# Attention passes of one width, ordered high before low, with two transposes of the second head moved between

## The chip, the cores and the metric

The kernel runs on one core of a Trainium2 chip. The metric is the device time of one execution in microseconds (us); lower is better. TensorE (PE) does matmuls and transposes, VectorE (DVE), ScalarE (ACT) and GpSimd (POOL) the elementwise work; SyncE (SP) issues most transfers.

## The reference

Eight sequences of 512 tokens by 256 channels go through a selective state-space layer (stage A of the kernel), then through attention whose value and output projections are sums over experts chosen by a gate (stage B), then through a feed-forward part and norms (stage C). The change is in stage B, which computes this, in float32:

```python
# x: (b, s, 256); 16 heads, 64 values a head, 8 experts of which 2 are kept
q = _rope(einsum('bsd,hdp->bhsp', x, Wq)); k = _rope(einsum('bsd,hdp->bhsp', x, Wk))
gv = _gate(x, Wsel_v)
v = einsum('bsd,bhse,hedp->bhsp', x, gv, Wv)
att = softmax(einsum('bhsp,bhtp->bhst', q, k) / sqrt(P), axis=-1)
o = einsum('bhst,bhtp->bhsp', att, v)
go = _gate(x, Wsel_o)
return einsum('bhsp,bhse,hepd->bsd', o, go, Wo)
```

## The kernel before

Every engine has its own program, written out by hand; semaphores tie them together, and each engine works strictly in the order of its own program. Stage B (`stage_b`, from line 875) runs 8 pairs of heads by 8 sequences, 64 batches. `turns` loops over them; `it` is the batch's number, `j` the pair and `b` the sequence. The last sequence of a pair also prepares the next pair's weights, and the first one comes right after them.

To keep float32 precision with a faster matmul type, each operand is split into a high part (rounded) and a low part (what rounding left). A product is three matmuls: high by high, high by low and low by high (`product`, L1156 to L1158). ScalarE makes the high parts and VectorE or GpSimd the low ones, always after the high one.

One batch, in TensorE's order (`batch`, L1255): the values of both heads' experts (`values`) mixed with the scores (`scores`); the transposes of head 0's exponentiated scores, four groups of four 128x128 transposes (`turn_probabilities`, L1200, groups n = 0 to 3, one PSUM bank each); head 0's attention (`attend`, L1210); head 1's transposes, n = 4 to 7, in the same four banks; the transposes of the output gates (`turn_gates`); head 1's attention; eight gate matmuls (`spread_gates`, L1233) with the next batch's raw query and key projection between them (`project_raw`); and 48 matmuls of output projection (`project`). The first gate matmul waits for the gates' low part (`low_gates`, L1462). The output projection waits for the low part of the first gated output, which GpSimd makes (`low_outputs`, L1060).

Attention of a head is four key chunks c, each with a high and a low pass over 512 queries. `vv` holds a head's values per chunk: 64 columns of high parts, then 64 of low parts. The high pass (L1219) has all 128 columns as weights and streams the high part of the probabilities, so its bank holds high by high on partitions 0 to 63 and low by high on 64 to 127. The low pass (L1221, for the last chunk L1218 and ahead of the high pass) has the 64 high columns and streams the low part. `attend` waits once per chunk, for the chunk's low part. Then ScalarE moves one half of the bank beside the other (`move_part`, L1342, into `aside`), and VectorE adds them (`add_parts`, L1469, into `oT`). Only then do the outputs of both heads get their gates (`gate_outputs`, L1478), go to ScalarE for the high part (L1353) and to GpSimd for the low part.

The order around this on the other engines: ScalarE does the high copies of head 0 (`high_probabilities`, L1331, n = 0 to 3), the next batch's input (`high_x`), head 1's values (`high_values`, L1325), `move_part` of head 0, then the high copies of head 1 (n = 4 to 7), the gates' high part (L1335) and `move_part` of head 1. VectorE does the gated values, the low parts of head 0 (`low_probabilities`, L1454), the output gates, `add_parts` of head 0, the low parts of head 1, `low_gates`, `add_parts` of head 1 and the gated outputs. A copy of head 1 into the ring of four chunks waits for the pass that read the old chunk (`pv_psum`).

Of the kernel before, what the change touches and what calls it, by code (L numbers as in the profile page):

```python
# [15 lines left out]
F32, F32R = mybir.dt.float32, mybir.dt.float32r  # L16
ALU = mybir.AluOpType
ACT = mybir.ActivationFunctionType
AX = mybir.AxisListType

P = 128
NB, S, D = 8, 512, 256
TT = S // P
# [6 lines left out]
H, E, HP, F = 16, 8, 64, 1024  # L30
# [844 lines left out]
def stage_b(nc, d, const, acc):  # L875
# [6 lines left out]
    with ExitStack() as ctx:  # L882
        def sb(name, shape, dtype=F32):
            return ctx.enter_context(nc.sbuf_tensor(name, shape, dtype))
# [7 lines left out]
        ps = ctx.enter_context(nc.psum_tensor("ps_b", [P, 8, S], F32))  # L892
# [23 lines left out]
        qk_full = sb("qk_full", [P, 2, S])  # L916
# [1 line left out]
        vg = sb("vg", [P, TT, E, HP])  # L918

        v4 = qk_full[:, :, :].rearrange("p a s -> p (a s)").rearrange("p (t e n) -> p t e n", t=TT, e=E // 2)  # L920
        oT, aside = sb("oT", [P, S]), sb("aside", [P, S])
        v2 = sb("v2", [P, TT, E // 4, HP])
        v = sb("v", [P, 2, TT, HP])
        vv = sb("vv", [P, 2, TT, 2 * HP], F32R)
        negmax = sb("negmax", [P, TT, 2])
        total = sb("total", [P, 2, TT])
        share = sb("share", [P, 2, TT])
# [3 lines left out]
        RING = 4  # L931
        probT = parts("probT", [P, RING, S])
# [5 lines left out]
        consts_loaded, consts_done, zero_done = sem("consts_b_loaded"), sem("consts_b_done"), sem("zero_done")  # L938
# [6 lines left out]
        v_psum, vg_done, vsum_done = sem("v_psum"), sem("vg_done"), sem("vsum_done")  # L945
        v_high, v_low = sem("v_high"), sem("v_low")
# [66 lines left out]
        def turns(eng, start, batch, pair_start=None):  # L1013

            def pair(j, more):
                if pair_start:
                    pair_start(j)
                with eng.Fori(0, NB - 1) as b:
                    batch(j * NB + b, j, b, True, False)
                batch(j * NB + (NB - 1), j, NB - 1, False, more)  # L1020

            start()
            with eng.Fori(0, PAIRS - 1) as j:
                pair(j, True)
            pair(PAIRS - 1, False)

        @block.gpsimd
        def _(pool):
            def low_x(it):
                pool.wait_ge(xT_high, it + 1)  # L1030
                pool.tensor_tensor(xT[1][:, :, :], xT_in[:, :, :], xT[0][:, :, :].bitcast(F32), ALU.subtract).then_inc(xT_low, 1)
# [20 lines left out]

            def low_values(it, h):
                pool.wait_ge(v_high, it * 2 + h + 1)
                pool.tensor_tensor(vv[:, h, :, HP:2 * HP], v[:, h, :, :], vv[:, h, :, 0:HP].bitcast(F32), ALU.subtract).then_inc(v_low, 1)

            def low_outputs(it, e):

# [85 lines left out]
                    rank_four(it + 1, ahead)  # L1144

            pool.memset(out_gate[:, :, :], 0.0).then_inc(zero_done, 1)
            low_x(0)

            pool.dma_start(acc[:, :, :, :], d["xT"].rearrange("b p k s -> p b k s")).then_inc(acc_loaded, 16)
# [3 lines left out]
        def _(pe):  # L1153
# [39 lines left out]
            def turn_probabilities(it, n):  # L1193
                h, c = divmod(n, TT)
                if n in (0, 3):
                    pe.wait_ge(exp_done, it * 2 * TT + (7 if n == 0 else 8))
                elif n >= 4:
                    pe.wait_ge(pT_low, it * N + n - 3)
                for t in range(TT):
                    mm = pe.transpose(ps[:, c, t * P:(t + 1) * P], prob[h][:, t, c * P:(c + 1) * P], ident[:, :])  # L1200
                mm.then_inc(pT_psum, 1)
# [5 lines left out]
                    mm = pe.transpose(ps[:, GT_BANK, t * P:(t + 1) * P], out_gate[:, t, :], ident[:, :])  # L1207
                mm.then_inc(gT_psum, 1)

            def attend(it, h, c):  # L1210

                if c == 0:
                    pe.wait_ge(v_low, it * 2 + h + 1)
                n = h * TT + c
                pe.wait_ge(pT_low, it * N + n + 1)
                bank, last = ATTEND_BANK[h], c == TT - 1
                if last:
                    pe.matmul(ps[0:HP, bank, :], vv[:, h, c, 0:HP], probT[1][:, n % RING, :], start=False, stop=False)  # L1218
                mm = pe.matmul(ps[:, bank, :], vv[:, h, c, :], probT[0][:, n % RING, :], start=(c == 0), stop=last)  # L1219
                if not last:  # L1220
                    mm = pe.matmul(ps[0:HP, bank, :], vv[:, h, c, 0:HP], probT[1][:, n % RING, :], start=False, stop=False)  # L1221
                mm.then_inc(pv_psum, 1)

            def spread_gates(it, p):

# [29 lines left out]
            def batch(it, j, b, more, more_pairs):  # L1255
                pe.wait_ge(w_low["wv"], j * 2 + 2)
                values(it, 0, 0)
                values(it, 0, 1)
                scores(it, 0)
                scores(it, 1)  # L1260
                values(it, 0, 2)
                values(it, 0, 3)
                values(it, 1, 0)
                scores(it, 2)
                scores(it, 3)
                values(it, 1, 1)
                values(it, 1, 2)
                values(it, 1, 3)
                for n in range(TT):
                    turn_probabilities(it, n)  # L1270
                for c in range(TT):
                    attend(it, 0, c)
                for n in range(TT, N):
                    turn_probabilities(it, n)
                turn_gates(it)
                for c in range(TT):
                    attend(it, 1, c)
                spread_gates(it, 0)
                spread_gates(it, 1)
                if more or more_pairs:  # L1280
                    if more_pairs:
                        pe.wait_ge(w_low["wqk"], j + 2)
                    project_raw(it + 1, 0)
                spread_gates(it, 2)
                if more or more_pairs:
                    project_raw(it + 1, 1)
                spread_gates(it, 3)
                for n in range(N):
                    project(it, j, n)

            pe.wait_ge(consts_done, 1)
            turns(pe, start, batch)

        @block.scalar
        def _(act):
# [26 lines left out]

            def high_values(it, h):
                act.wait_ge(vsum_done, CREDIT + it * VSUM + h * 6 + 6)
                act.activation(vv[:, h, :, 0:HP], v[:, h, :, :], ACT.Copy).then_inc(v_high, 1)  # L1325

            def high_probabilities(it, n):
                act.wait_ge(pT_psum, it * N + n + 1)
# [8 lines left out]
            def move_part(it, h):  # L1337

                act.wait_ge(pv_psum, it * N + h * TT + TT)
                act.wait_ge(oT_done, it * 2 + h)  # L1340
                here, other = slice(h * HP, (h + 1) * HP), slice((1 - h) * HP, (2 - h) * HP)
                act.activation(aside[here, :], ps[other, ATTEND_BANK[h], :], ACT.Copy).then_inc(part_moved, 1)  # L1342

# [59 lines left out]
        def _(dve):  # L1403
# [12 lines left out]
            def rotate(it):  # L1416

                dve.wait_ge(vsum_done, CREDIT + it * VSUM)
                dve.wait_ge(rot_done, it * 3 + 3)
                dve.tensor_tensor(qk_full[:, :, :], rot[:, 0:2, :], rot[:, 2:4, :], ALU.add).then_inc(qk_done, 1)  # L1420

# [134 lines left out]

            dve.wait_ge(tables_loaded, 32)
            dve.wait_ge(consts_done, 1)
            dve.wait_ge(zero_done, 1)
            turns(dve, start, batch)  # L1560


# [397 lines left out]
```

## Time and profile before

| what | value |
|---|---|
| median of 3 runs (lowest, highest) | 4069.31 us (4068.82, 4069.96) |
| the profiled execution's own time | 4069.74 us |
| its span, first to last instruction | 4067.9 us |
| TensorE busy, mean granted clock | 3706.3 us (91%), 0.972 |
| VectorE busy | 3307.9 us (81%) |
| GpSimd busy | 2717.1 us (67%) |
| ScalarE busy | 1962.4 us (48%) |

How to read it: busy time is the time in which an engine has an instruction in work. Matmuls overlap (a 512-column matmul is recorded as 0.39 us but the next one starts 0.23 later), so starts tell more than durations. A timeline row gives the start in us from the beginning, the duration (of a run of equal instructions, from the first start to the last end), the engine (PEld is TensorE's weight load), the line, the operation, output<-inputs, shapes and the count; in brackets the idle time before it and what ended it.

### The profile page before, as it was taken

The page shows a single profiled execution, that of the slowest core. Times are in us where ns is not written, and L with a number is a line of the kernel's source. Part 1 is how long each engine was busy: PE and PEld are TensorE (multiplying, and loading weights), DVE is VectorE, ACT ScalarE, POOL GpSimd, SP SyncE. Part 2 cuts the span into 40 slices and gives each one's busy share as a digit, 9 for nine tenths or more (in the row PEclk, how much of TensorE's full clock was granted, in tenths as well). Part 3 has the DMA queues.
Part 4 walks back from the last instruction along what each step waited for, and adds up shares of the span by engine and source line. Part 5 has one row for each costly group of instructions (what it writes and reads, how often), then busy time and mean ns, then how long its engine had stood idle before and what let it go on. Part 6 is the DMA issues. An engine that isn't in the chain of part 4 may idle for free. (4 is left out here: it accounts for less than half of the span.)

```text
span 4067.9 us, 55014 instructions
## 1 busy us (share of the span) xinstructions
PE 3706.3 (91%) x16000; PEld 2539.0 (62%) x16000; DVE 3307.9 (81%) x3879; ACT 1962.4 (48%) x3646; POOL 2717.1 (67%) x2844
## 2 busy tenths in 40 slices
PE   6888988888649999999999999999999999999786
PEld 2344434443337777777777777777777777777675
DVE  5999999999928787878787878778788778787698
ACT  4645664566324444454445454545454445444443
POOL 3767776777636677667667667667667667766354
PEclk9999999999969999999999999999999999999898
DMA  2101110111030001001001001001000000000111
GB/s 75 52 37 37 63 68 37 37 62 63 21 134 16 10 16 39 15 15 39 13 18 37 12 10 44 15 10 44 10 15 17 37 10 21 11 15 10 33 41 36
DMA packets 53667, 131.92 MB, mean 32 GB/s; under 512 B 4223, under 2 KB 33791, under 8 KB 47073
## 3 DMA queue, kind: packets, MB, share of 16 engines
q1 hardware_dynamic: 52560, 127.02, 8.7%
q0 software_dynamic: 1040, 4.19, 0.3%
q8 instruction: 20, 0.33, 0.0%
q14 instruction: 47, 0.38, 0.0%
HBM read 114.16 MB, written 17.04 MB: 32 GB/s over the span
## 5 line engine op out<-in xcount | busy, mean ns | idle before, releaser
L371 POOL TENSOR_TENSOR state<-state,c_rows 128x1024 f32<-128x1024 f32 x256 | 604.1, 2363 | 266.8 <-DVE state L790 265.5
L1320 ACT ACTIVATE prob<-ps_b,negmax 128x512 f32<-128x512 f32 x512 | 345.8, 686 | 653.1 <-DVE negmax L1439 653.1
L790 DVE TENSOR_TENSOR_SCAN state<-dA,ps_a 128x1024 f32<-128x1024 f32 x256 | 584.6, 2284 | 29.9 <-PE ps_a L503 7.9
L503 PE MATMUL ps_a<-state,ident 128*128 128x512 f32 x1024 | 504.7, 617 | 70.9 <-DVE yz L802 70.5
L666 ACT ACTIVATE dA<-dt,a_neg 128x511 f32<-128x511 f32 x512 | 338.7, 712 | 452.3 <-DVE state L790 451.9
L1433 DVE TENSOR_TENSOR vg<-ps_b,gates 128x1024 f32<-128x1024 f32 x256 | 313.4, 1224 | 251.7 <-PE ps_b L1158 239.7
L1047 POOL TENSOR_TENSOR qk_full<-vg 128x512 f32<-128x512 f32 x256 | 329.4, 1287 | 254.2 <-DVE vg L1433 254.2
L1060 POOL TENSOR_TENSOR ogT_low<-prob,ogT_high 128x512 fp32r<-128x512 f32 x256 | 324.3, 1302 | 207.5 <-ACT ogT_high L1353 207.5
L1156 PE MATMUL ps_b<-ogT_high,wo_high 128*128 128x512 f32 x1024 | 412.9, 403 | 11.1 <-DVE ogT_low L1485 10.8
L1156 PE MATMUL ps_b<-wv_high,xT_high 128*128 128x512 f32 x1024 | 414.0, 404 | 0.0
L1158 PE MATMUL ps_b<-ogT_high,wo_low 128*128 128x512 f32 x1024 | 404.2, 395 | 0.0
L1157 PE MATMUL ps_b<-ogT_low,wo_high 128*128 128x512 f32 x1024 | 402.0, 393 | 0.0
L1157 PE MATMUL ps_b<-wv_low,xT_high 128*128 128x512 f32 x1024 | 400.9, 391 | 0.0
L1158 PE MATMUL ps_b<-wv_high,xT_low 128*128 128x512 f32 x1024 | 399.2, 390 | 0.0
L503 PEld LDWEIGHTS ps_a<-state,ident 128*128 128x128 f32 x1024 | 199.1, 197 | 286.5 <-issue 195.1
L1439 DVE TENSOR_REDUCE negmax<-ps_b 128x2 f32<-128x1024 f32 x256 | 300.9, 1217 | 62.8 <-PE ps_b L1189 62.8
L781 DVE TENSOR_TENSOR ps_a<-du,ps_a 128x1024 f32<-128x1024 f32 x256 | 314.6, 1229 | 29.5 <-DVE state L790 4.1
L1454 DVE TENSOR_TENSOR probT_low<-ps_b,probT_high 128x512 fp32r<-128x512 f32 x512 | 316.2, 676 | 2.2 <-ACT probT_high L1331 2.2
L1331 ACT ACTIVATE probT_high<-ps_b 128x512 fp32r<-128x512 f32 x512 | 264.6, 604 | 62.0 <-PE ps_b L1200 59.9
L1353 ACT ACTIVATE ogT_high<-ps_b 128x512 fp32r<-128x512 f32 x256 | 153.1, 598 | 240.6 <-PE ps_b L1158 240.6
L1219 PE MATMUL ps_b<-probT_high,vv 128*128 128x512 f32 x512 | 242.4, 473 | 22.1 <-DVE probT_low L1454 21.4
L1200 PE MATMUL ps_b<-ident,prob 128*128 128x128 f32 x2048 | 244.7, 273 | 2.3 <-ACT prob L1320 2.3
(233 smaller groups left out, 8571.3 us busy)
## 6 DMA issues: line engine op xcount, KB each, us to landing
xT<-xT_scratch SPq DMA_DIRECT2D x65, 512.0 KB, 3.3
c_rows<-c_scratch SPq DMA_DIRECT2D x32, 1024.0 KB, 5.5
wv<-in_wv SPq DMA_DIRECT2D x8, 1024.0 KB, 4.9
wo<-in_wo SPq DMA_DIRECT2D x8, 1024.0 KB, 7.0
x_in<-in_x SPq DMA_DIRECT2D x8, 512.0 KB, 4.8
x_a<-in_x SPq DMA_DIRECT2D x8, 512.0 KB, 7.2
x_scratch<-x_a SPq DMA_DIRECT2D x8, 512.0 KB, 2.8
xT_scratch<-x2T SPq DMA_DIRECT2D x8, 512.0 KB, 2.7
```

The lines of the kernel that those rows point to most:

```text
L371: pool.tensor_tensor(state, state, c_rows[:, n, :].unsqueeze(1).to_broadcast([P, HALF, S]), ALU.mult).then_inc(hc_done, 1)
L503: mm = pe.matmul(ps[:, Y_BANK + m, :], ident[:, :], h[s % RING][:, m, :], start=(n == 0), stop=(n == NS - 1))
L666: act.activation(dA[s % RING][:, m, 1:S], dt[par][:, HALF * f + m, 1:S], ACT.Exp, scale=a_neg[:, HALF * f + m, n:n + 1]).then_inc(dA_done, 1)
L781: dve.tensor_tensor(ps[:, DBX_BANK:DBX_BANK + HALF, :], half(du[par], f), ps[:, B_BANK + s % 2, :].unsqueeze(1).to_broadcast([P, HALF, S]) ...
L790: dve.tensor_tensor_scan(h[s % RING][:, :, :].rearrange("p c s -> p (c s)"), dA[s % RING][:, :, :].rearrange("p c s -> p (c s)"), ps[:, DB ...
L1047: pool.tensor_tensor(v4[:, at, :, :], vg[:, at, 0:4, :], vg[:, at, 4:8, :], ALU.add).then_inc(vsum_done, 1)
L1060: pool.tensor_tensor(ogT[1][:, e, :], og[:, e, :], ogT[0][:, e, :].bitcast(F32), ALU.subtract).then_inc(oT_low0, 1)
L1156: pe.matmul(out, left(0), right(0), start=start, stop=False)
L1157: pe.matmul(out, left(0), right(1), start=False, stop=False)
L1158: return pe.matmul(out, left(1), right(0), start=False, stop=stop)
L1320: act.activation(prob[h][:, t, :], ps[:, score_bank(t) + h, :], ACT.Exp, bias=negmax[:, t, h:h + 1], accum_out=total[:, h, t:t + 1]).then_ ...
L1454: dve.tensor_tensor(probT[1][:, n % RING, :], ps[:, n % TT, :], probT[0][:, n % RING, :].bitcast(F32), ALU.subtract).then_inc(pT_low, 1)
```

## The change

`attend` is split in two. `attend_high` runs a head's four high passes, each after a wait for its high copy alone; `attend_low` then runs the four low passes, each after a wait for its low part. `vv` is now 192 columns per chunk: low parts, high parts, and zeros that GpSimd writes once at the start. The high pass takes columns 0 to 127, the low pass 64 to 191, so both have 128 columns of weights; the low pass adds its product on partitions 0 to 63 and zero on the others. The counter that releases ScalarE's `move_part` and the ring's copies (`pv_psum`) now counts low passes.

TensorE's order becomes: high passes of head 0, transposes n = 4 and 5, low passes of head 0, transposes n = 6 and 7, gate transposes, high and low passes of head 1. Because the high passes no longer wait for VectorE, a wait for the gated values that share their bank (`vg_done`) is added. `aside` becomes the second half of `qk_full`; for that, VectorE's `rotate` gets a wait for the additions done, and ScalarE's `move_part` waits only for those of the batch before.

```diff
-        oT, aside = sb("oT", [P, S]), sb("aside", [P, S])
+        oT, aside = sb("oT", [P, S]), qk_full[:, 1, :]
-        vv = sb("vv", [P, 2, TT, 2 * HP], F32R)
+        vv = sb("vv", [P, 2, TT, 3 * HP], F32R)
...
-                pool.tensor_tensor(vv[:, h, :, HP:2 * HP], v[:, h, :, :], vv[:, h, :, 0:HP].bitcast(F32), ALU.subtract).then_inc(v_low, 1)
+                pool.tensor_tensor(vv[:, h, :, 0:HP], v[:, h, :, :], vv[:, h, :, HP:2 * HP].bitcast(F32), ALU.subtract).then_inc(v_low, 1)
...
+            pool.memset(vv[:, :, :, 2 * HP:3 * HP].bitcast(F32), 0.0).then_inc(zero_done, 1)
...
-            def attend(it, h, c):
-
-                if c == 0:
-                    pe.wait_ge(v_low, it * 2 + h + 1)
-                n = h * TT + c
-                pe.wait_ge(pT_low, it * N + n + 1)
-                bank, last = ATTEND_BANK[h], c == TT - 1
-                if last:
-                    pe.matmul(ps[0:HP, bank, :], vv[:, h, c, 0:HP], probT[1][:, n % RING, :], start=False, stop=False)
-                mm = pe.matmul(ps[:, bank, :], vv[:, h, c, :], probT[0][:, n % RING, :], start=(c == 0), stop=last)
-                if not last:
-                    mm = pe.matmul(ps[0:HP, bank, :], vv[:, h, c, 0:HP], probT[1][:, n % RING, :], start=False, stop=False)
-                mm.then_inc(pv_psum, 1)
+            def attend_high(it, h):
+
+                pe.wait_ge(v_low, it * 2 + h + 1)
+                pe.wait_ge(vg_done, it * 4 + 3)
+                for c in range(TT):
+                    pe.wait_ge(pT_high, it * N + h * TT + c + 1)
+                    pe.matmul(ps[:, ATTEND_BANK[h], :], vv[:, h, c, 0:2 * HP], probT[0][:, c % RING, :], start=(c == 0), stop=False)
+
+            def attend_low(it, h):
+
+                for c in range(TT):
+                    pe.wait_ge(pT_low, it * N + h * TT + c + 1)
+                    pe.matmul(ps[:, ATTEND_BANK[h], :], vv[:, h, c, HP:3 * HP], probT[1][:, c % RING, :], start=False,
+                              stop=(c == TT - 1)).then_inc(pv_psum, 1)
...
-                for c in range(TT):
-                    attend(it, 0, c)
-                for n in range(TT, N):
-                    turn_probabilities(it, n)
+                attend_high(it, 0)
+                turn_probabilities(it, TT)
+                turn_probabilities(it, TT + 1)
+                attend_low(it, 0)
+                turn_probabilities(it, TT + 2)
+                turn_probabilities(it, TT + 3)
                 turn_gates(it)
-                for c in range(TT):
-                    attend(it, 1, c)
+                attend_high(it, 1)
+                attend_low(it, 1)
...
+            pe.wait_ge(zero_done, 2)
...
-                act.activation(vv[:, h, :, 0:HP], v[:, h, :, :], ACT.Copy).then_inc(v_high, 1)
+                act.activation(vv[:, h, :, HP:2 * HP], v[:, h, :, :], ACT.Copy).then_inc(v_high, 1)
...
-                act.wait_ge(oT_done, it * 2 + h)
+                act.wait_ge(oT_done, it * 2)
...
+                dve.wait_ge(oT_done, it * 2)
...
-            dve.wait_ge(zero_done, 1)
+            dve.wait_ge(zero_done, 2)
```

## Rows read from the trace of the kernel before

**Rows 1.** Stage B's stretch: length, busy PE PEld DVE ACT POOL, granted clock, DMA.

```profile
1191.00:3807.00 2616.00, 2552.91 (x12304) 1896.55 (x12304) 2072.14 (x2643) 1243.81 (x2541) 1804.27 (x2140) 0.99 0.06 22
```

**Rows 2.** The page's groups of instructions: busy us, mean ns of one.

```profile
L1454 DVE TENSOR_TENSOR probT_low<-ps_b,probT_high 128x512 fp32r<-128x512 f32 x512 | 316.2, 676 | 2.2 <-ACT probT_high L1331 2.2
L1331 ACT ACTIVATE probT_high<-ps_b 128x512 fp32r<-128x512 f32 x512 | 264.6, 604 | 62.0 <-PE ps_b L1200 59.9
L1200 PE MATMUL ps_b<-ident,prob 128*128 128x128 f32 x2048 | 244.7, 273 | 2.3 <-ACT prob L1320 2.3
```

**Rows 3.** Timeline of one batch, TensorE from its first transposes to the gate matmuls.

```profile
2023.78 1.91 PE L1200 MATMUL ps_b<-ident,prob 128*128 128x128 f32 x16
...
2025.92 0.49 PE L1219 MATMUL ps_b<-probT_high,vv 128*128 128x512 f32 x1 [0.24 <-DVE probT_low L1454]
...
2026.26 0.39 PE L1221 MATMUL ps_b<-probT_low,vv 128*64 128x512 f32 x1
...
2027.72 0.44 PE L1218 MATMUL ps_b<-probT_low,vv 128*64 128x512 f32 x1
2027.77 0.19 PEld L1219 LDWEIGHTS ps_b<-probT_high,vv 128*128 128x128 f32 x1
...
2028.00 0.39 PE L1219 MATMUL ps_b<-probT_high,vv 128*128 128x512 f32 x1
...
2030.57 0.51 PE L1219 MATMUL ps_b<-probT_high,vv 128*128 128x512 f32 x1
...
2032.66 0.39 PE L1219 MATMUL ps_b<-probT_high,vv 128*128 128x512 f32 x1
...
2033.09 1.21 PE L1233 MATMUL ps_b<-gT,spread 128*128 128x512 f32 x4
```

**Rows 4.** The same timeline, VectorE and ScalarE.

```profile
2024.41 2.07 ACT L1331 ACTIVATE probT_high<-ps_b 128x512 fp32r<-128x512 f32 x4 [1.05 <-PE ps_b L1200]
2025.19 2.47 DVE L1454 TENSOR_TENSOR probT_low<-ps_b,probT_high 128x512 fp32r<-128x512 f32 x4
...
2028.07 0.42 ACT L1325 ACTIVATE vv<-v 128x256 fp32r<-128x256 f32 x1 [0.65 <-POOL v L1051]
...
2028.52 0.59 ACT L1342 ACTIVATE aside<-ps_b 64x512 f32<-64x512 f32 x1
...
2029.85 2.47 DVE L1454 TENSOR_TENSOR probT_low<-ps_b,probT_high 128x512 fp32r<-128x512 f32 x4
...
2032.34 0.69 DVE L1462 TENSOR_TENSOR gT<-ps_b,gT 16x512 fp32r<-16x512 f32 x1
...
2033.16 0.59 ACT L1342 ACTIVATE aside<-ps_b 64x512 f32<-64x512 f32 x1 [1.47 <-PE ps_b L1219]
```

**Rows 5.** The same batch, up to its output projection: GpSimd, then TensorE.

```profile
2036.48 1.29 POOL L1060 TENSOR_TENSOR ogT_low<-prob,ogT_high 128x512 fp32r<-128x512 f32 x1 [3.21 <-ACT ogT_high L1353]
...
2037.36 0.63 PE L1233 MATMUL ps_b<-gT,spread 128*128 128x512 f32 x2
...
2037.92 0.47 PE L1156 MATMUL ps_b<-ogT_high,wo_high 128*128 128x512 f32 x1
```

**Rows 6.** Timeline, TensorE's first matmul behind score matmuls of 64 rows.

```profile
2013.68 0.50 PE L1156 MATMUL ps_b<-wv_high,xT_high 128*128 128x512 f32 x1
```

**Rows 7.** Timeline of GpSimd where stage B starts.

```profile
1161.61 0.52 POOL L1146 MEMSET out_gate<- 128x512 f32 x1 [14.76 <-POOLq L170]
1168.34 2.34 POOL L1031 TENSOR_TENSOR xT_low<-xT,xT_high 128x1024 fp32r<-128x1024 f32 x1 [6.20 <-ACT xT_high L1299]
```

**Rows 8.** Timeline of a pair's first batch: head 0's last pass, ScalarE's value copy.

```profile
2836.56 0.39 PE L1219 MATMUL ps_b<-probT_high,vv 128*128 128x512 f32 x1
...
2837.75 0.42 ACT L1325 ACTIVATE vv<-v 128x256 fp32r<-128x256 f32 x1 [0.68 <-POOL v L1051]
```

**Rows 9.** Waits of TensorE in stage B: who for whom, total us, times, longest.

```profile
PE ps_b L1219 <- DVE probT_low L1454: 21.4, 64, 1.1
PE ps_b L1156 <- DVE ogT_low L1485: 10.8, 7, 1.6
```

## The prediction

> **What bounds the kernel now.** I read the sums by stretch first, then the timeline of one batch of stage B, then the waits. Stage B is 2616 of the 4067.9 us, and in it TensorE is busy 2553 us at a granted clock of 0.99 (the 2.4 GHz level) [rows 1]. It runs 64 batches, nearly all alike; I take the one whose probability transposes start at 2023.78. The busy share says "TensorE-bound", but the attention passes, the part that is edited, are not. The 16 transposes take 0.109 us each ((1.91 - 0.273) / 15), so TensorE is free at 2025.53, yet the first pass of head 0 starts at 2025.92; from there three pairs of passes take 1.80 us, 0.60 each [rows 2, 3]. VectorE's four low parts stand 0.598 apart ((2.47 - 0.676) / 3), from 2025.19 [rows 4]. A pair starts 0.73 after its low part does, that is 0.06 after it ends. So VectorE sets the pace, and head 1 shows the same: low part at 2029.85, pass at 2030.57 [rows 3, 4].
>
> The reader is to see one chain in rows 3 and 4. Last pass of head 0 at 2028.00; ScalarE moves the part at 2028.52; VectorE adds it and makes four low parts from 2029.85, the last at 31.64, and the gates' low part at 32.34; the gate matmuls start at 33.09. TensorE has slack inside this chain and none after it: gate matmuls and raw projections are back to back up to the pair at 2037.36, and the output projection at 2037.92 is only 0.09 later than the engine would be free, since it also waits for GpSimd's part of 2036.48 [rows 5]. After that TensorE has no idle time worth naming until the next transposes. So what the edit does to the start of the output projection, it does to the batch.
>
> **The change, part by part.**
>
> *Equal width.* Before, the low passes use 64 columns, now 128. The eight passes of a head stay eight. A 128-column pass that follows a matmul directly costs 0.235 (the four gate matmuls take 1.21, less 0.40 for the last and 0.34 for the released first, by 2). The wide pass at 2025.92 that had to wait is followed by the next after 0.34: 0.107 more, because its weights were held by the same wait. The narrow pass at 2027.72 waited too and is followed after 0.28, 0.05 more, half the columns; and the weights of the wide pass behind it begin to load at 2027.77, beneath it [rows 3]. Nothing is left over for the change of width: the sum counts 0 for it. The other end is that all time over 8 x 0.235 = 1.88 in the two stretches (2028.00 + 0.235 - 2025.92 = 2.31 and 2033.09 - 2030.57 = 2.52) is its price; that is the first rival.
>
> The Trainium skill, page "TensorEngine Tiling (Array Packing)", section Key Properties, says that changing the tiling mode drains TensorE, and so speaks for this edit. The trace agrees where the row side of the tile changes: the first 128-row matmul behind the 64-row score matmuls, at 2013.68, takes 0.50, like a pass released late, with nothing to wait for [rows 6]. It doesn't for the column side, by the 0.28 above. By the rule the sum would be the first rival's.
>
> *New order in head 0.* Four high passes, each once ScalarE's copy is there. The copies start at 2024.41 and (2.07 - 0.604) / 3 = 0.489 apart, and end at 25.01, 25.50, 25.99 and 26.48 [rows 4]. How fast TensorE sees a ScalarE copy the trace hardly shows; bounds are 0 and the 0.15 from GpSimd's end (2036.48 + 1.29 = 37.77) to 37.92 [rows 5]; I take VectorE's 0.06. So the passes start at 25.53, 25.76, 26.04 and 26.53, the last exposing its weights: free at 26.87. Then two groups of head 1's transposes, 8 x 0.109 = 0.87: 27.74. (They need low parts 1 and 2, seen by 25.92 and 26.52.) Then four low passes, at 27.74, 27.97, 28.20 and 28.43; the last needs the low part seen at 27.72, so no wait is left. Before, the last pass stood at 2028.00. ScalarE follows the last pass by 0.50 (32.66 to 33.16 in head 1), so at 28.93 in place of 28.52: **+0.41**. It can't come out below about 0: ScalarE's copy of the second head's values ends at 28.07 + 0.42 = 28.49 just ahead of that step, whatever TensorE does [rows 4]. That is why moving work to fill TensorE's wait has nothing to win here.
>
> *Who waits.* Head 1's copies are queued behind this step on ScalarE, and its low parts behind the addition on VectorE. The low parts, the gates' low part and the gate matmuls all come 0.41 later: gate matmuls at 33.50. TensorE passes the time with transposes 6 and 7, the gates' transposes and head 1's high passes (paced by copies from about 29.54), all before the last low part. From 33.50 the old density holds: last gate matmul at 37.59 + 0.41 = 38.00, output projection at 38.235. Since TensorE is now last there, the 0.09 vanishes: **+0.31**.
>
> *Head 1's end.* The last low part starts at 31.64 + 0.41, and the one pass left behind it at 32.79 (two before, to 32.66). It ends after 0.50, at 33.29, against 32.66 + 0.39 = 33.05: +0.24 for the second addition, the gated outputs and GpSimd's part, which would put the projection at 38.16. Not last.
>
> *Small things.* The 512-column fill is one more of the 0.52 us fill that GpSimd does before it idles 6.2 us for ScalarE's copy: 0 [rows 7]. The added waits of VectorE before the rotation, and TensorE's for zeros and for the second head's gated values, are for steps long done in batch order: 0; uncovered, they would cost at most the 0.15 between a release and its matmul, bounded above. ScalarE's relaxed wait is not the late one: 0. The side tile's new place changes no order: it is written after GpSimd's last sum (that value copy waits for it). No DMA and nothing of SP's is moved.
>
> *Sum over batches.* Two kinds differ. In the first batch of seven weight pairs GpSimd is late: ScalarE's value copy ends 2837.75 + 0.42 = 38.17, while the new last pass (the old one's 2836.56 + 0.43, and 0.50) would let it go at 37.49: hidden, 0 [rows 8]. That there are seven follows from TensorE's 64 waits before a high pass: 57 like the 0.24 at 2025.92 and 7 of the longest kind, 1.1, make the row's 21.4 us [rows 3, 9]. In the last batch of seven pairs the projection waits on VectorE's low outputs anyway (10.8 us, 7 times), which go by the other chain: +0.24; the very last batch has no raw projection to be late with: +0.24. So 49 x 0.31 + 8 x 0.24 = 15.2 + 1.9 = **17.1 us**. The profiled execution took 4069.74 in all (span 4067.9), 0.43 above the median of the runs. 4069.7 + 17.1 = 4086.8; by the median 4086.4. I say 4086.5.
>
> *Its own bounds.* Low: no exposed weights (0.107) and copies seen at once (0.06): 0.14 a batch, 7 us. High: copies seen after 0.15 (+0.09) and the 0.09 before the projection not absorbed: 49 x 0.49 + 8 x 0.33 = 27 us. So 4076 to 4096.
>
> **The rivals.**
>
> *Faster: the width was the price.* If both stretches shrink to 1.88, (0.43 + 0.64) x 64 = 68 us: 4001. It decides from the point where head 0's last pass starts before 2028.00. Against it stand the pairs' 0.60, equal to VectorE's 0.598, the 0.28, and ScalarE's 28.49. A part of it would need those engines faster too. Chance 0.06.
>
> *No change: the delay is absorbed.* This is the lower bound or less: the high passes all preload, copies are seen at once, and a further few hundredths go in the slack between the two chains; under 0.13 a batch, 4069 to 4077. For it: both chains stand within 0.1 us of TensorE. Against: 0.41 is four times that. Chance 0.12.
>
> *Much slower: every pass with a wait of its own exposes its weights.* Where one wait served a pair, each pass now has one. If weights aren't fetched past a wait although it is fulfilled, four low passes cost 4 x 0.107 = 0.43 more on the chain: 0.74 a batch, 49 x 0.74 + 8 x 0.67 = 42 us, 4111. Against it: transposes behind fulfilled waits run unbroken, 16 in 1.91. Chance 0.10.
>
> The Trainium skill's page "TensorE: Matmul & The Clock Gate", section LDWEIGHTS, has the load's time go by columns, 53 ns for 64 and 107 for 128. By it the four widened loads would add 4 x 0.054 = 0.21 us a head if exposed, part of this last rival.
>
> **How the numbers follow.** Forecast 0.72, faster 0.06, no change 0.12, much slower 0.10. A measurement of this kernel tells about 0.2% (8 us) from no change, so to 4077.5. Forecast and last rival are slower: 0.82; same 0.12; faster 0.06. The forecast's own range, 4076 to 4096, holds 0.72 at most; down to 4070 it takes in most of the middle case and leaves 0.2 out.
>
> **What would show it.** In the profile of the changed kernel, from a batch's first transpose: last high pass of head 0 after 2.75 us; last low pass after 4.65 (before 4.22); ScalarE's move after 5.15 (4.74); gate matmuls after 9.72 (9.31); output projection after 14.45 (14.14); batches 0.31 longer, except first ones of a pair. All passes 0.39 long except those released late, 0.50. Wrong if head 0's last pass starts before 4.3, or if the gate matmuls come later than 9.9.

## The result, and the profile after

| | before | changed |
|---|---|---|
| median of 7 runs each (lowest, highest), us | 4068.82 (4066.64, 4071.98) | 4083.47 (4082.17, 4086.63) |
| the profiled execution's own time, us | 4069.74 | 4086.63 |
| its span, us | 4067.9 | 4084.8 |
| TensorE busy, mean granted clock | 3706.3 us, 0.972 | 3724.1 us, 0.972 |

The changed kernel is slower: ratio 1.0039, 95% interval 1.0028 to 1.0049, or 14.7 us by the medians. The forecast was 4086.5 us. All ratios and intervals here are worked out from the fast runs alone, and can differ by up to 0.0006 from the quotient of two medians.

The timeline of a batch of the changed kernel answers [rows 3 to 5]. Its first transposes start at 2031.57, so 7.79 us are to be taken off before comparing with the batch of before at 2023.78. TensorE first:

```profile
2031.57 1.91 PE L1201 MATMUL ps_b<-ident,prob 128*128 128x128 f32 x16
...
2034.32 0.51 PE L1217 MATMUL ps_b<-probT_high,vv 128*128 128x512 f32 x1
2034.66 1.04 PE L1201 MATMUL ps_b<-ident,prob 128*128 128x128 f32 x8
2035.46 1.18 PE L1223 MATMUL ps_b<-probT_low,vv 128*128 128x512 f32 x4
...
2041.32 1.20 PE L1235 MATMUL ps_b<-gT,spread 128*128 128x512 f32 x4 [0.23 <-DVE gT L1468]
...
2045.60 0.63 PE L1235 MATMUL ps_b<-gT,spread 128*128 128x512 f32 x2
2046.07 0.40 PE L1157 MATMUL ps_b<-ogT_high,wo_high 128*128 128x512 f32 x1
```

The last high pass of head 0 (L1217) stands 2.75 us after the first transpose, then come the eight transposes that were moved, then the low passes (L1223). The last of these starts 0.39 before the group's end, at 2036.25, 4.68 after the first transpose; before it was 4.22. The other engines in the same view:

```profile
2035.86 0.42 ACT L1330 ACTIVATE vv<-v 128x256 fp32r<-128x256 f32 x1 [0.64 <-POOL v L1051]
...
2036.75 0.60 ACT L1347 ACTIVATE qk_full<-ps_b 64x512 f32<-64x512 f32 x1 [0.47 <-PE ps_b L1223]
...
2037.37 2.07 ACT L1336 ACTIVATE probT_high<-ps_b 128x512 fp32r<-128x512 f32 x4
...
2037.47 0.68 DVE L1475 TENSOR_TENSOR oT<-ps_b,qk_full 64x512 f32<-64x512 f32 x1 [1.24 <-ACT qk_full L1347]
...
2038.08 2.47 DVE L1460 TENSOR_TENSOR probT_low<-ps_b,probT_high 128x512 fp32r<-128x512 f32 x4
...
2040.58 0.69 DVE L1468 TENSOR_TENSOR gT<-ps_b,gT 16x512 fp32r<-16x512 f32 x1
...
2041.13 0.59 ACT L1347 ACTIVATE qk_full<-ps_b 64x512 f32<-64x512 f32 x1 [1.21 <-PE ps_b L1223]
...
2044.53 5.07 POOL L1060 TENSOR_TENSOR ogT_low<-prob,ogT_high 128x512 fp32r<-128x512 f32 x4 [3.48 <-ACT ogT_high L1358]
```

ScalarE's move (L1347) now idles 0.47 for TensorE behind the value copy; before it followed that copy at once [rows 4]. The steps of the chain behind it keep their distances. From the first transpose:

| step | before | forecast | changed |
|---|---|---|---|
| last high pass of head 0 | - | 2.75 | 2.75 |
| last pass of head 0 | 4.22 | 4.65 | 4.68 |
| ScalarE's move of head 0 | 4.74 | 5.15 | 5.18 |
| first low part of head 1 | 6.07 | 6.48 | 6.51 |
| gate matmuls | 9.31 | 9.72 | 9.75 |
| ScalarE's move of head 1 | 9.38 | 9.62 | 9.56 |
| output projection | 14.14 | 14.45 | 14.50 |
| plain batch, start to start | 39.95 | 40.26 | 40.25 |

The waits of TensorE in stage B, who for whom, in total, times, longest; this answers [rows 9]:

```profile
PE ps_b L1235 <- DVE gT L1468: 14.1, 64, 0.2
PE ps_b L1157 <- DVE ogT_low L1491: 11.0, 8, 1.6
```

Of the 21.4 us that TensorE idled before high passes, 4.4 us in seven batches are left, and TensorE is fuller inside the stretch. In their place every batch has an idle 0.23 before the gate matmuls. The wait went down and the time went up: what was hidden by TensorE's slack is now on the chain.

### The profile page after: what moved, and what is told of

Read it like the earlier page. It is cut to its first block and busy times, and to the rows that moved or that the text cites. A ratio compares the mean times of both kernels' runs of the same rounds, so it can differ in the third digit from the quotient of the medians.

```text
span 4084.8 us, 55142 instructions
## 1 busy us (share of the span) xinstructions
PE 3724.1 (91%) x16000; PEld 2585.6 (63%) x16000; DVE 3319.1 (81%) x3879; ACT 1958.7 (48%) x3646; POOL 2719.9 (67%) x2845
## 5 line engine op out<-in xcount | busy, mean ns | idle before, releaser
L1201 PE MATMUL ps_b<-ident,prob 128*128 128x128 f32 x2048 | 255.2, 273 | 2.3 <-ACT prob L1325 2.3
L1201 PEld LDWEIGHTS ps_b<-ident,prob 128*128 128x128 f32 x2048 | 234.8, 140 | 25.9 <-ACT prob L1325 5.3
```

## The experiments

Times are in the order of the runs. "Plain batch" is the distance from one batch's first transpose to the next one's, for batches that are neither first nor last of a weight pair.

| kernel | TensorE's order in head 0 | move of head 0 | plain batch | ratio to before (95%) |
|---|---|---|---|---|
| before | pairs, then transposes | early | 39.95 | 1 |
| changed | high, 2 groups, low | early | 40.25 | 1.0039 (1.0028 to 1.0049) |
| `e1_wide_only` | as before, 128 wide | early | 40.07 | 1.0020 (1.0011 to 1.0029) |
| `e2_none_moved` | high, low | early | 39.80 | 0.9973 (0.9963 to 0.9983) |
| `e4_one_moved` | high, 1 group, low | early | 39.82 | 0.9973 (0.9964 to 0.9983) |
| `e3_narrow_three` | as changed, 64 wide | early | 40.24 | 1.0039 (1.0026 to 1.0053) |
| `e5_three_moved` | high, 3 groups, low | early | 40.68 | 1.0102 (1.0087 to 1.0117) |
| `e7_before_one_moved` | pairs, 1 group before the last | early | 40.32 | 1.0048 (1.0033 to 1.0063) |
| `e8_move_late` | as changed | late | 39.21 | 0.9890 (0.9875 to 0.9906) |
| `e9_none_moved_move_late` | high, low | late | 39.54 | 0.9935 (0.9922 to 0.9949) |
| `e11_before_move_late` | as before | late | 40.24 | 1.0039 (1.0025 to 1.0053) |
| `e12_copy_first_two` | as changed | late, a copy first | 39.28 | 0.9889 (0.9873 to 0.9904) |
| `e13_before_late_relaxed` | as before | late, wait relaxed | 39.71 | 0.9958 (0.9944 to 0.9971) |

**The width alone.** The kernel before, with wide low passes. All that the width needs comes with it: the zero columns, the new place of `aside`, and with that place the added wait of VectorE and the relaxed one of ScalarE.

```diff
-                    pe.matmul(ps[0:HP, bank, :], vv[:, h, c, 0:HP], probT[1][:, n % RING, :], start=False, stop=False)
+                    pe.matmul(ps[:, bank, :], vv[:, h, c, HP:3 * HP], probT[1][:, n % RING, :], start=False, stop=False)
...
-                    mm = pe.matmul(ps[0:HP, bank, :], vv[:, h, c, 0:HP], probT[1][:, n % RING, :], start=False, stop=False)
+                    mm = pe.matmul(ps[:, bank, :], vv[:, h, c, HP:3 * HP], probT[1][:, n % RING, :], start=False, stop=False)
```

> The kernel before with only the low passes widened from 64 to 128 columns (and the zero columns and the side tile's place that this needs); the order of passes and transposes is untouched. My theory: width frees nothing, and the last chunk's low pass, released late, exposes a load of 128 columns instead of 64, 0.05 us more in each head. In a batch: last pass of head 0 4.27 after the first transpose (4.22 before), ScalarE's move +0.05, the end of head 1 +0.10, so +0.05 to +0.10 a batch, 3 to 6 us slower than before: ratio 1.001. Rival 'the width was the price' (the drain at a change of tile): pairs of passes closer than 0.60 and up to 68 us faster, ratio down to 0.983. Third: exactly no change, if the load is never exposed.

It is 8.3 us slower by the medians (4075.88 to 4067.54), with an interval from 4 to 12. Its timeline, one batch (first transpose 2023.54):

```profile
2027.47 0.50 PE L1219 MATMUL ps_b<-probT_low,vv 128*128 128x512 f32 x1
...
2028.33 0.59 ACT L1344 ACTIVATE qk_full<-ps_b 64x512 f32<-64x512 f32 x1
```

The last chunk's low pass, released late, takes 0.50 where the narrow one took 0.44 [rows 3]: the wide load's other 0.05. ScalarE's move goes from 4.74 to 4.79 and the batch gets 0.11 longer, both heads' 0.05 added up. That is just past the top of the 0.05 to 0.10 expected, and the 8.3 us are above the 3 to 6; their interval reaches down into that range. The pairs keep their 0.60. The width frees nothing here; where a low pass is the one released last, it costs.

**The order alone.** The changed kernel with the two groups set back:

```diff
                 attend_high(it, 0)
-                turn_probabilities(it, TT)
-                turn_probabilities(it, TT + 1)
                 attend_low(it, 0)
+                turn_probabilities(it, TT)
+                turn_probabilities(it, TT + 1)
```

> The changed kernel with transposes 4 and 5 set back behind the low passes of head 0; high passes first and equal width stay. My theory: the two groups of transposes in front of the low passes are the whole loss. Last low pass of head 0 at 3.94 after the first transpose (released by its low part), ScalarE's move at 4.74 as before since its value copy ends there, gate matmuls at 9.31, end of head 1 0.18 earlier than before, projection at 14.05 (TensorE-bound): 0.09 less than before a batch, 6 us faster than before (ratio 0.9985) and 20 us faster than the changed kernel. Rival 'separate waits or the high passes cost': stays slower than before, ratio above 1.001.

4056.47 us, 11 us below before (6 were expected) and 27 us below the changed kernel. One batch (first transpose 2016.76), TensorE and ScalarE:

```profile
2019.84 1.35 PE L1223 MATMUL ps_b<-probT_low,vv 128*128 128x512 f32 x4
...
2021.04 0.42 ACT L1330 ACTIVATE vv<-v 128x256 fp32r<-128x256 f32 x1 [0.64 <-POOL v L1051]
2021.49 0.59 ACT L1347 ACTIVATE qk_full<-ps_b 64x512 f32<-64x512 f32 x1
...
2026.06 1.20 PE L1235 MATMUL ps_b<-gT,spread 128*128 128x512 f32 x4 [0.22 <-DVE gT L1468]
...
2030.80 0.40 PE L1157 MATMUL ps_b<-ogT_high,wo_high 128*128 128x512 f32 x1
```

The low passes end at 2021.19, yet the move comes at 4.73 as before: it follows the value copy. Gate matmuls at 9.30, projection at 14.04. So the two groups of transposes are the loss, and high passes first are a gain, since only one pass is left behind the last low part of head 1. The gain is 0.16 a batch and not 0.09: the projection's first matmul takes 0.40 where it took 0.47 [rows 5], as TensorE, no longer GpSimd, comes last and the weights are loaded by then. That 0.07 was not in my sum, and it makes up most of the difference between the 6 us expected and the 11 measured.

**One group, and three.** The same lines with one group ahead of `attend_low`, and with three.

> The changed kernel with one group of transposes (n = 4) ahead of head 0's low passes instead of two. My theory has a threshold: the last low pass comes at 4.23 and ends at 4.62, still ahead of ScalarE's value copy (4.71), so ScalarE's move stays at 4.74 and the batch is as with none moved: 6 us faster than before, ratio 0.9985. Rival 'each group moved costs its 0.44 us on TensorE': halfway between none and two moved, +0.15 a batch against none, some 4 us slower than before, ratio 1.001.

> The changed kernel with three groups of transposes (n = 4, 5, 6) ahead of head 0's low passes instead of two. My theory: past the threshold each group adds its 4 x 0.109 = 0.44 us to the chain through ScalarE's move. Last low pass of head 0 at 5.10, move at 5.61 (5.18 with two, 4.74 with one or none), gate matmuls at 10.18, batches 0.73 longer than before; 49 x 0.73 + 8 x 0.67 - 7 x 0.14 = 40 us slower than before, ratio 1.010. If the loss of the changed kernel were a fixed price of splitting the transposes, it would stay at 1.004.

With one group, 4057.54 us, ratio 0.9973, as with none; with three, 4106.59 us against 4066.77, ratio 1.0102, where 1.010 was expected. Two lines of the timeline with one group (first transpose 2018.47), then two of the kernel with three (2031.72):

```profile
2021.92 1.18 PE L1223 MATMUL ps_b<-probT_low,vv 128*128 128x512 f32 x4
...
2023.22 0.60 ACT L1347 ACTIVATE qk_full<-ps_b 64x512 f32<-64x512 f32 x1
```

```profile
2036.04 1.18 PE L1223 MATMUL ps_b<-probT_low,vv 128*128 128x512 f32 x4
...
2037.35 0.59 ACT L1347 ACTIVATE qk_full<-ps_b 64x512 f32<-64x512 f32 x1 [0.93 <-PE ps_b L1223]
```

The move stands at 4.73, 4.75, 5.18 and 5.63 with none, one, two and three groups. The first 0.44 is free. A part of it fills TensorE's own wait for the last low part (that pass starts at 3.94 with none and at 4.24 with one, 0.30 later and not 0.44), and the rest lies under the value copy, which ends at 4.71. With one group that room is nearly used up: the last pass ends at 4.63. From then on each group adds its 0.44 in full, and the idle time in brackets shows who is waited for. A price per group from the first on is out, and so is a fixed price of splitting.

**Narrow low passes in the new order.**

```diff
-                    pe.matmul(ps[:, ATTEND_BANK[h], :], vv[:, h, c, HP:3 * HP], probT[1][:, c % RING, :], start=False,
-                              stop=(c == TT - 1)).then_inc(pv_psum, 1)
+                    if c == TT - 1:
+                        pe.matmul(ps[:, ATTEND_BANK[h], :], vv[:, h, c, HP:3 * HP], probT[1][:, c % RING, :], start=False,
+                                  stop=True).then_inc(pv_psum, 1)
+                    else:
+                        pe.matmul(ps[0:HP, ATTEND_BANK[h], :], vv[:, h, c, HP:2 * HP], probT[1][:, c % RING, :], start=False,
+                                  stop=False).then_inc(pv_psum, 1)
```

> The changed kernel with the first three low passes of each head narrow again (64 columns); the last one stays 128 wide, as it closes the accumulation over all partitions. Order as in the changed kernel. My theory: width is worth nothing, the same as the changed kernel within 2 us, ratio to before 1.004, passes 0.235 apart. Rival 'a change of tile width drains': each head has two changes, some 0.1 us each by the score matmuls' case: +0.2 on the way to ScalarE's move, 10 us slower than the changed kernel, ratio 1.006.

4083.90 us beside the changed kernel's 4083.47. One batch (first transpose 2027.52):

```profile
2031.40 0.94 PE L1227 MATMUL ps_b<-probT_low,vv 128*64 128x512 f32 x3
...
2032.17 0.39 PE L1224 MATMUL ps_b<-probT_low,vv 128*128 128x512 f32 x1
2032.40 1.04 PE L1201 MATMUL ps_b<-ident,prob 128*128 128x128 f32 x8
```

The wide pass after three narrow ones starts 0.22 after the last (2031.95) and takes 0.39: no drain where only the columns of the tile change. By the page "TensorEngine Tiling (Array Packing)" of the Trainium skill, section "Key Properties", a switch of the tile mode needs a drain; the trace shows none between 64 and 128 columns.

**Transposes moved without the new passes.** The kernel before, with one group set between its third and fourth chunk:

```diff
-                for c in range(TT):
-                    attend(it, 0, c)
-                for n in range(TT, N):
+                for c in range(TT - 1):
+                    attend(it, 0, c)
+                turn_probabilities(it, TT)
+                attend(it, 0, TT - 1)
+                for n in range(TT + 1, N):
                     turn_probabilities(it, n)
```

> The kernel before, pairs and narrow low passes as they are, with one group of transposes (n = 4) set between head 0's third and fourth chunk. It has neither the equal width nor the high passes first. My theory: in this order TensorE comes to the last chunk just as its low part is there, so even one group is too many: last pass of head 0 at 4.58 (4.22 before), ScalarE's move at 5.08 (4.74), batches 0.34 longer, 57 x 0.34 = 19 us slower than before, ratio 1.005. If transposes alone do no harm without the changed passes: ratio 1.000.

4085.70 us against 4066.77, 19 us slower, as worked out. One batch (first transpose 2027.04):

```profile
2031.62 0.40 PE L1219 MATMUL ps_b<-probT_high,vv 128*128 128x512 f32 x1
...
2032.14 0.60 ACT L1344 ACTIVATE aside<-ps_b 64x512 f32<-64x512 f32 x1 [0.38 <-PE ps_b L1219]
```

The last pass is at 4.58 and the move at 5.10, so it is the same chain that is delayed. Here a single group is too much, as nothing was saved ahead of it.

**The queue behind the move.** If the delay hurts only because head 1's copies stand behind head 0's move, then taking the move out of their way must free the moved transposes. TensorE's program stays that of the changed kernel; two other engines change:

```diff
                 high_values(it, 1)
-                move_part(it, 0)
                 for n in range(TT, N):
                     high_probabilities(it, n)
                 high_gates(it)
+                move_part(it, 0)
                 move_part(it, 1)
...
-                add_parts(it, 0)
                 for n in range(TT, N):
                     low_probabilities(it, n)
                 low_gates(it)
+                add_parts(it, 0)
                 add_parts(it, 1)
```

> The changed kernel, TensorE's program untouched, with head 0's move on ScalarE and its addition on VectorE set behind head 1's copies, low parts and the gates' low part. My theory: the moved transposes hurt only because head 1's copies are queued behind head 0's move. Without that, copies of head 1 start at 4.73 after the first transpose (5.80 in the changed kernel), low parts at 5.43 (6.51), the last pass of head 1 at 7.95 (9.03), gate matmuls at 8.67 (9.75), TensorE-bound projection at 13.41 (14.50): about 0.8 a batch less than before, some 50 us faster than before, ratio 0.988. Rival 'the transposes' place costs on TensorE itself': stays at or above 1.00.

> The kernel with none of the transposes moved, and head 0's move and addition set late as in the run with the late move. My theory: the sign of the reordering turns. Copies of head 1 now wait for their transposes, 4.92 in place of 4.73, the last low part starts at 7.40 in place of 7.22, gate matmuls at 8.84 in place of 8.67, projection at 13.58: 0.62 a batch less than before, 40 us faster than before (ratio 0.990), so 11 us slower than the late move with two groups moved, where with the early move it is 27 us faster. If the transposes' place is harmful as such, this one is the faster of the two.

4022.73 us with the changed order (44 us faster, some 50 expected) and 4040.01 us with none moved, against 4066.77: the late move turns the sign of what the moved transposes do. One batch of the first (first transpose 2007.84):

```profile
2011.72 1.18 PE L1223 MATMUL ps_b<-probT_low,vv 128*128 128x512 f32 x4
...
2012.11 0.42 ACT L1330 ACTIVATE vv<-v 128x256 fp32r<-128x256 f32 x1 [0.63 <-POOL v L1051]
...
2012.44 2.04 ACT L1336 ACTIVATE probT_high<-ps_b 128x512 fp32r<-128x512 f32 x4
...
2013.05 2.48 DVE L1460 TENSOR_TENSOR probT_low<-ps_b,probT_high 128x512 fp32r<-128x512 f32 x4 [0.55 <-ACT probT_high L1336]
...
2016.28 1.41 DVE L1475 TENSOR_TENSOR oT<-ps_b,qk_full 64x512 f32<-64x512 f32 x2
2016.31 0.76 PEld L1235 LDWEIGHTS ps_b<-gT,spread 128*128 128x128 f32 x4 [0.53 <-DVE gT L1468]
...
2021.23 0.47 PE L1157 MATMUL ps_b<-ogT_high,wo_high 128*128 128x512 f32 x1
```

Head 0's last pass is as late as in the changed kernel (4.67), but head 1's copies start at 4.60 (5.80 there), gate matmuls are at 8.47 (9.75), the projection at 13.39 (14.50). The copies came 0.13 and the low parts 0.22 earlier than I had said. The batch gained 0.74 and not 0.8, since the projection waits for GpSimd again (0.47 long): VectorE's two additions (L1475) now stand in line, 0.72 apart. With none moved, the copies have to wait for their transposes:

```profile
2016.92 2.06 ACT L1336 ACTIVATE probT_high<-ps_b 128x512 fp32r<-128x512 f32 x4 [0.20 <-PE ps_b L1201]
...
2020.81 1.20 PE L1235 MATMUL ps_b<-gT,spread 128*128 128x512 f32 x4 [0.22 <-DVE gT L1468]
```

That is 4.90 and 8.79 after its first transpose (2012.02). Its gain of 27 us fell short of the 40 expected: the projection is at 13.71, held by GpSimd and not by TensorE, by the same additions.

**The old order with the late move.** To complete the square, the same two moves in the kernel before.

> The kernel before, TensorE's program untouched, with head 0's move on ScalarE and its addition on VectorE set late, as in the run with the late move. It completes a square: TensorE's old or new order, move early or late. My theory: head 1's copies then wait for their transposes (5.08 after the first transpose, against 5.36 before and 4.60 with the new order), the last low part starts at 7.50 (7.86 before, 7.02 with the new order), gate matmuls at 8.95, projection at 13.87: 0.27 a batch less than before in most batches, more in the seven first ones, 21 us faster than before, ratio 0.995. So the new order is worth 24 us more with the late move and costs 16 us with the early one. If the late move alone explained the whole gain, this run would be at 0.989 too.

It came out 14 us slower, ratio 1.0039, where 21 us faster was expected: a plain miss. Its copies (5.09), low parts and gate matmuls (8.98) stand where they were expected. One batch (first transpose 2024.69), VectorE and ScalarE:

```profile
2033.65 0.68 DVE L1469 TENSOR_TENSOR oT<-ps_b,aside 64x512 f32<-64x512 f32 x1
...
2034.36 0.59 ACT L1342 ACTIVATE aside<-ps_b 64x512 f32<-64x512 f32 x1 [1.40 <-DVE oT L1469]
```

The bracket names it: ScalarE's second move waits 1.40 for VectorE's first addition of its own batch. That wait is in the kernel before (`oT_done`, `it * 2 + h`), and the changed kernel relaxes it. I had costed it at nothing. With the early move the rows agree, as the second move waits for TensorE there and not for the addition [rows 4], but no run relaxed it alone. With the late one it puts both additions and both moves in one line. The next run relaxes it and nothing else:

```diff
-                act.wait_ge(oT_done, it * 2 + h)
+                act.wait_ge(oT_done, it * 2)
```

> The run that set the move late in the kernel before (TensorE's old order), with ScalarE's move of head 1 relaxed as in the changed kernel: it waits for the additions of the batch before, not for head 0's addition of its own batch. In the run without this, ScalarE's second move stood at 9.67 after the first transpose, just after the first addition (8.95 + 0.68), where the last pass (8.54) would have let it go at 9.05. My theory: the second move goes back to 9.05, the second addition to 9.77 (10.29), the projection to 13.90 (14.42), 0.5 a batch less, some 33 us: ratio to before 0.996. If something else held the second move, the ratio stays at 1.004.

4050.39 us against 4066.61, ratio 0.9958. One batch (first transpose 2015.04):

```profile
2024.01 0.59 ACT L1342 ACTIVATE aside<-ps_b 64x512 f32<-64x512 f32 x1 [0.71 <-PE ps_b L1219]
...
2028.92 0.47 PE L1156 MATMUL ps_b<-ogT_high,wo_high 128*128 128x512 f32 x1
```

The second move is back at 8.97 and waits for TensorE; the projection is at 13.88. So the square is, as ratios to before: old order 1 and 0.9958, changed order 1.0039 and 0.9890, with the move early and late. The changed order costs 0.4% with the early move and gives 0.7% with the late one. "Order" here is the whole change to TensorE's program, width and high passes first included; the two groups of transposes by themselves cost 27 us with the early move (0.9973 to 1.0039) and win 17 with the late one (0.9935 to 0.9890).

**A copy set ahead.** The late move, and head 1's first copy ahead of the value copy:

```diff
                 high_x(it + 1)
+                high_probabilities(it, TT)
                 high_values(it, 1)
-                for n in range(TT, N):
+                for n in range(TT + 1, N):
                     high_probabilities(it, n)
```

> The changed kernel with the late move, and head 1's first copy on ScalarE (n = 4) also set ahead of its value copy (it waits only for the first low pass of head 0, seen at about 4.4 after the first transpose). My theory: the chain now begins with that copy, and VectorE's low parts are 0.598 apart from there: first low part at 5.0 (5.21), last at 6.8 (7.02), gate matmuls at 8.27 (8.47), and 0.2 a batch less than with the late move, 12 us: ratio 0.986. It wins nothing if the value copy, now later, holds up GpSimd's part and with it head 1's high passes past 6.13.

4019.86 us, ratio 0.9889: no difference from the late move (0.9890) that can be told. One batch (first transpose 2006.47):

```profile
2010.94 0.60 ACT L1336 ACTIVATE probT_high<-ps_b 128x512 fp32r<-128x512 f32 x1 [0.83 <-PE ps_b L1223]
...
2011.43 0.41 ACT L1330 ACTIVATE vv<-v 128x256 fp32r<-128x256 f32 x1
...
2011.57 2.68 DVE L1461 TENSOR_TENSOR probT_low<-ps_b,probT_high 128x512 fp32r<-128x512 f32 x4 [0.43 <-ACT probT_high L1336]
...
2011.74 1.56 ACT L1336 ACTIVATE probT_high<-ps_b 128x512 fp32r<-128x512 f32 x3
```

The first copy came as hoped (4.47), but I had let the low parts run 0.598 apart from it. The other three copies stand behind the value copy, from 5.27 on, and VectorE's four take 2.68 for 2.48: the last low part starts at 7.10, later than the 7.02 it replaces. Plain batches are 0.07 longer. The first batches of a pair, where GpSimd brings the values late, are 39.67 for 40.28: there the copy no longer waits for them. The two cancel.

## Why the prediction was right

**The sum.** The forecast was +17.1 us, the medians say +14.7 and the spans +16.9, of which the last is near by chance. From the first transposes of batch 1 to those of batch 64 the traces have 2541.7 and 2557.2 us: +15.5, where the forecast has 16.9 for these 63 batches. In it are 14.1 from 48 plain batches, 0.8 from batch 1, -1.0 from the seven first ones and 1.6 from the seven last ones; the misses of the two middle terms partly cancel. Of the span's other 1.4 (rounded), 2.4 lie ahead of those transposes and -0.9 behind the last; the start of stage B shifts that much between kernels whose code there is the same (first transposes at 1212.5 to 1220.0 in the thirteen profiles), so it is no part of the change.

**Equal width: 0, right** for the forecast's order; shown by the narrow passes in the new order (0.22 and 0.39, no cost, no gain). It has a price where the wide low pass is the one released last: +0.11 a batch in the old order, about half from each head.

**New order in head 0: +0.41, measured +0.44.** The assumption behind it, that TensorE sees a ScalarE copy 0.06 after its end, held: the last high pass stands 2.75 after the first transpose, the copy ends at 2.69. Behind it two small errors cancel: the first low pass starts at 3.89, not 3.96, but the last one 0.79 later (1.18 - 0.39), not the 0.70 of three steps of 0.235. The floor held too: with none or one group the move stays at 4.73 and 4.75. The sentence built on it, that moving work into TensorE's wait has nothing to win here, holds for this queue order alone. With the move late the same transposes win 17 us (0.9890 against 0.9935).

**Who waits: +0.31, right in its sum and off in two parts.** The projection starts 0.36 later where I had 0.31 (0.03 from the longer chain, the rest from gate matmuls and raw projections, 4.75 apart where I took 4.74), but its weights are now loaded in time and it takes 0.40, not 0.47 [rows 5]; I had counted the 0.09 of waiting and not this 0.07. Together about +0.30, as measured; that the sum came out so near is in part luck.

**Head 1's end: +0.24, measured +0.18 at the second addition and +0.26 at GpSimd's part.** It is not last, as forecast. The last pass ends 0.26 later. ScalarE's second move then follows it sooner (0.03 after its end, 0.11 before), but ScalarE's first gated output follows VectorE's later (0.11 after its end, 0.03 before), and GpSimd's part starts at 12.96 for 12.70. The sooner move stands in all ten profiles with ScalarE's relaxed wait, the later one in the kernel before and in `e7_before_one_moved`, which have the strict wait; the two steps offset each other, and why they shift was not tried.

**Batches of other kinds.** Last ones of a pair: forecast +0.24, measured +0.23. First ones: forecast 0, measured -0.15 (40.85 for 41.00): the delay is hidden as said, but the end of head 1 comes 0.25 earlier and the projection's weights are ready, a gain that I left out. Batch 1 got 0.80 longer: its projection meets a wait for VectorE's low outputs, the eighth beside the seven of before.

**The rivals.** "The width was the price" and with it the drain for columns fall by the width alone and by the narrow passes. "Every pass with a wait of its own exposes its weights" falls by the row of four low passes in 1.18: they start 0.31, 0.24 and 0.23 apart, where a load exposed each time would make it 0.34. "The delay is absorbed" falls by the batch's 0.30, and the two runs with none and one group show where it would have held.

## What to carry to other kernels

Ask of a step that waits not how long it waits but what stands behind it in the next engine's queue: here, of 0.87 us of transposes the first 0.44 were free and the second 0.44 charged in full, since ScalarE and VectorE held the second head's work behind the first head's result. Before filling an engine's gap with work of its own, take what isn't needed soon out of the queue that feeds the chain; after that the same filling pays. Moving the two groups took 0.9973 to 1.0039 with the early move and 0.9935 to 0.9890 with the late one, and the version with the late move beats both kernels. A wait costed at nothing is so for one order only: give it a new price when queues are reordered.

## What the runs showed of the hardware

Whether a step of ScalarE or VectorE overlaps with the one in front of it goes, in these rows, by the partition at which its operands start. ScalarE starts a copy over all 128 partitions 0.33 us after the value copy in front of it starts (2012.11 to 2012.44 in the late move), though that copy is recorded as 0.42 long. The move of head 0 reads partitions 64 to 127 and writes 0 to 63; it starts 0.45 after the value copy (2021.04 to 2021.49), past its end, also where TensorE had long finished.

VectorE's full-width parts follow each other after 0.60. In the changed kernel the addition of head 0, on partitions 0 to 63, is followed by the first full-width low part after 0.61 (2037.47 to 2038.08), before its end, so half the width does not hold up the next step. The gates' low part lies on partitions 64 to 79 and starts 0.70 after the last low part (2039.88 to 2040.58), past its end. The two additions of the late move start at partitions 0 and 64 and stand 0.72 apart (1.41 - 0.69), again without overlap. On VectorE none of these steps shifts partitions, so a shift isn't needed for it. No run changed the starting partition alone. By how much a shorter step between the two additions would bring the projection forward wasn't tried either.
